# Three moves in a transformer block: first masks, gate rows and first residual each in another place

## Chip, cores and metric

The kernel runs on one core of a Trainium2 chip. The core has a matrix engine (TensorE, "PE"; its weight loads are shown apart as "PEld"), a vector engine (VectorE, "DVE"), a scalar engine (ScalarE, "ACT"), GpSimd ("POOL") and SyncE ("SP"), which here only issues DMAs. Each engine runs its own program; they wait for each other through semaphores. The metric is the device time of one execution in microseconds, as the median of several runs.

## What is computed

One transformer block with layer norm behind each half, on x of 2 sequences x 2048 tokens x 512 features: multi-query causal attention (16 heads of 32, one key and value head), then a mixture of eight experts of which each token takes two.

```python
qkv = einsum('bsd,ed->bse', x, Wqkv_w) + Wqkv_b      # q: 16 heads of 32, k and v: one head each
scores = einsum('bqhd,bkd->bhqk', q, k) / sqrt(32)   # causal mask, softmax over k
out = einsum('bsd,ed->bse', softmax(scores) @ v, out_w) + out_b
x = layernorm(x + out)
top2 = top_k(x @ router_w.T, 2)                      # softmax over the two scores
h = silu(xb @ w1[e]) * (xb @ w3[e])                  # bf16, 8 experts, 128 wide
x = layernorm(x + sum over the two of  weight * (h @ w2[e]))
```

## The kernel before, in words

**Blocks and tiles.** A sequence is worked off in four blocks of 512 tokens (g = 0 to 3), so the program has eight blocks. A block has an attention stage, then an output projection with the first layer norm, in between which the queries, keys and values of the next block are projected, then routing and an expert stage. In attention, a tile is 128 queries of all 16 heads against 128 keys. `TILES` lists them, 136 in a sequence: for query group q first the tile on the diagonal (`FIRST[q]`), which needs the causal mask, then the others. In the first block the tiles are q = 0 (one tile), q = 1 (two), q = 2 (three) and q = 3 (four).

**One tile.** TensorE makes the scores, two halves of two matmuls each, into three PSUM pairs that are used in turn (L1184). ScalarE makes the exponential of each half (L653). GpSimd zeroes both halves of a diagonal tile (`mask`, L520). Two tiles later TensorE multiplies with the values (`times_values`, L1206; the profile has two records for each of its four matmuls, so one tile shows as x8). VectorE adds up a group's tiles (`add`, L833), TensorE forms the denominators from the sums with ones (L1224), VectorE transposes and inverts them and scales the context (`normalise_context`, L882 to L892). ScalarE and VectorE split each context into a high and a low part (L665, L901) for the fp32 products of the output projection (L1037).

**Who waits where, between the sequences.** At a sequence's end VectorE adds the residuals of the last block (`finish_experts`: L906, then statistics L909 and L910), counts `mv_ready`, and waits for GpSimd's reciprocal deviations (`make_rstd`, L545 and L547) to normalise (L916) and so let SyncE store (L434). TensorE meanwhile starts the next sequence: the first tile's scores, then, once the fourth residual is added, the second's and third's, then the first product with the values, which waits for both halves of the first mask. GpSimd's program is a loop over the two sequences (`pool.Fori`); the last `make_rstd` of a sequence is the last thing in its body, so it stands ahead of the next sequence's masks. Its waits in the loop are against register values. The other places where the program asks whether there is a next sequence are branches.

**At a block's end.** TensorE's order is: the last products with the values, output projection of the block's first 128 tokens (`project_out(g, 0)`), the last denominators, projections 1 and 2, keys and values of the next block (L1044, L1049; they wait for GpSimd's low part of x, L565), projection 3, and the queries of the next block. VectorE's order is: the outstanding low parts, `normalise_context` of the last group, its low part, then `finish_attention` with the residuals 0 to 3. Around the attention of a block TensorE has a branch (on a bound that decides whether the scores need a shift); between projection 0 and the last denominators it jumps over the part not taken.

**The expert stage.** TensorE makes two up projections of each of eight experts (`up`, eight matmuls of L1327), turns the gates (L1357), and, once ScalarE has copied them (L689), spreads each expert's row over the partitions (`gate_rows`, one matmul of L1335, two banks in turn). ScalarE applies silu (L683), VectorE multiplies the two projections (`times_linear`, L948, counts `prod_done`), then by the gate row (L995, counts `h_done`). VectorE's order is: products 0 to 3, gated products 0, 1, 2, product 4, gated 3, product 5, gated 4, product 6, gated 5, product 7, gated 6, gated 7. `up` of expert e waits for product e - 3, a gate row for the gated product two before it. The first down projections (`down`, L1342) of the first five experts (`EARLY`) for two token tiles stand in the stage; the others (`LATE`, and all of token tiles 2 and 3) follow behind the next block's first scores, or at once in a sequence's last block. The next block's scores wait for all eight products (`prod_done`), its first exponential for all eight gated products (`h_done`).

## Time and profile before

| | before |
|---|---|
| median of 3 runs | 1117.82 us (1116.93 to 1120.11) |
| the profiled execution | 1121.4 us, span 1119.7 us |
| mean granted TensorE clock | 0.993 |
| PE, busy | 1079.0 us, 96% |
| PEld | 520.2 us, 46% |
| DVE | 888.6 us, 79% |
| ACT | 713.4 us, 64% |
| POOL | 199.3 us, 18% |
| chain of work that ended last | PE 75%, DVE 12%, issue 5% |

Times in the rows are microseconds from the span's start. A row of the timeline has start, duration, engine, line, operation, tile written and tiles read, count, and in brackets the idle time ahead of it with what ended it. Neighbouring operations of one line are merged. "issue" is time in which an engine waited for nothing that the profile shows. The granted clock is a share of 2.4 GHz; 0.50 is the lower level, 1.2 GHz.

### The profile page before, as it was taken

Reading aid. Unit: us, or ns where it says so; the run is one execution under the profiler, and the core shown is the slowest. Engines: PE = TensorE matmul, PEld = TensorE weight load, DVE = VectorE, ACT = ScalarE, POOL = GpSimd, SP = SyncE. Lnnn points to the kernel's source line nnn. Section 1 sums busy time; section 2 is a strip of 40 time slices with the busy share of each in tenths; the row PEclk is TensorE's granted clock in tenths of the full one; section 3 lists DMA queues with packets and bytes.
Section 4 is the critical chain, followed back from the end, with each engine's and each line's share of the span. In section 5 each row is a group of like instructions: output and inputs, shape, how many; then the busy total and the mean of one; then the engine's idle time right before and its main releaser. Section 6 shows DMA issues by size and latency. Waiting matters only on the chain.

```text
span 1119.7 us, 17340 instructions
## 1 busy us (share of the span) xinstructions
PE 1079.0 (96%) x5970; PEld 520.2 (46%) x5994; DVE 888.6 (79%) x1101; ACT 713.4 (64%) x844; POOL 199.3 (18%) x162
## 2 busy tenths in 40 slices
PE   8999999999999999999989999999999999999996
PEld 6365435543337433335634643474333654333462
DVE  4566899779976699987667679976998767898956
ACT  6734785478864498885445457644888447888821
POOL 3520332013110120111032013301211201211000
PEclk9999999999999999999989999999999999999999
DMA  4976401442001622001352353016400152200001
GB/s 146 208 114 141 124 1 40 106 121 38 2 2 53 137 76 38 1 1 39 78 136 75 75 131 76 2 52 138 113 1 1 39 126 65 38 1 2 1 1 38
DMA packets 40331, 72.19 MB, mean 64 GB/s; under 512 B 13969, under 2 KB 14993, under 8 KB 40209
## 3 DMA queue, kind: packets, MB, share of 16 engines
q1 hardware_dynamic: 24624, 56.64, 19.1%
q0 software_dynamic: 13584, 11.54, 7.1%
q10 hardware_dynamic: 2000, 2.51, 0.7%
q8 instruction: 62, 1.02, 0.4%
q14 instruction: 61, 0.49, 0.1%
HBM read 25.58 MB, written 8.39 MB: 30 GB/s over the span
## 4 chain that ended last, share of the span: by engine, by line
PE 75%; DVE 12%; issue 5%; ACT 2%; POOL 2%; DMA 1%; SPq 1%; DVEq 0%; ACTq 0%; POOLq 0%
PE sc L1184 21%; PE bank L1206 19%; PE sc L1037 8%; PE bank L1037 7%; PE sc L1327 7%; DVE psum_k L833 5%; PE sc L1224 3%; PE sc L1342 2%; PE bank L1224 2%; DVE stats L909 2%; POOL prob L520 1%; DVE res L906 1%; PE bank L1335 1%; PE sc L1271 1%; PE bank L1342 1%
## 5 line engine op out<-in xcount | busy, mean ns | idle before, releaser
L653 ACT ACTIVATE prob<-sc 128x1024 f32<-128x1024 f32 x544 | 525.5, 1025 | 133.7 <-PE sc L1184 133.5
L833 DVE TENSOR_TENSOR psum_k<-psum_k,prob 128x2048 f32<-128x2048 f32 x170 | 403.4, 2373 | 4.7
L1184 PE MATMUL sc<-q_st,k_st 128*128 128x512 f32 x1088 | 327.1, 422 | 8.0 <-DVE rden L882 3.8
L1184 PEld LDWEIGHTS sc<-q_st,k_st 128*128 128x128 f32 x1088 | 183.7, 188 | 249.7 <-ACT prob L653 177.3
L1206 PE MATMUL bank<-prob,v_sb 128*32 128x512 f32 x2176 | 288.2, 607 | 3.3 <-POOL prob L520 3.3
L520 POOL TENSOR_SCALAR_AFFINE_SELECT prob<-prob 128x1024 f32<-128x1024 f32 x64 | 112.4, 1798 | 527.7 <-ACT prob L653 527.7
L1327 PE MATMUL sc<-prob,w_sb 128*128 128x512 bf16 x503 | 117.3, 379 | 1.3 <-issue 1.3
L1206 PEld LDWEIGHTS bank<-prob,v_sb 128*32 128x32 f32 x2176 | 44.5, 108 | 107.4 <-issue 89.4
L683 ACT ACTIVATE prob<-sc 128x512 f32<-128x512 f32 x64 | 38.0, 594 | 73.0 <-PE sc L1327 72.9
L833 DVE TENSOR_TENSOR psum_k<-prob 128x2048 f32<-128x2048 f32 x28 | 64.0, 2286 | 20.7 <-POOL prob L520 17.1
L1037 PE MATMUL bank<-q_st,wq_hi 128*128 128x512 f32 x240 | 80.3, 399 | 0.0
L1327 PEld LDWEIGHTS sc<-prob,w_sb 128*128 128x128 bf16 x512 | 49.5, 99 | 62.6 <-issue 5.9
L665 ACT ACTIVATE q_hi<-ctxn 128x512 fp32r<-128x512 f32 x32 | 20.2, 633 | 64.6 <-DVE ctxn L892 64.6
L565 POOL TENSOR_TENSOR q_st<-res,q_st 128x2048 fp32r<-128x2048 f32 x7 | 34.8, 4968 | 126.3 <-ACT q_st L670 126.2
L948 DVE TENSOR_TENSOR prob<-sc,prob 128x512 f32<-128x512 f32 x64 | 43.5, 681 | 12.8 <-ACT prob L683 11.8
L995 DVE TENSOR_TENSOR psum_k<-bank,prob 128x512 bf16<-128x512 f32 x64 | 42.6, 685 | 13.6 <-PE bank L1335 13.6
L1037 PE MATMUL sc<-ow_hi,q_hi 128*128 128x512 f32 x128 | 52.8, 413 | 0.0
L906 DVE TENSOR_TENSOR res<-sc,res 128x512 f32<-128x512 f32 x48 | 32.3, 673 | 24.9 <-PE sc L1342 10.6
L1037 PE MATMUL sc<-ow_hi,q_lo 128*128 128x512 f32 x128 | 51.0, 398 | 0.0
L1037 PE MATMUL sc<-ow_lo,q_hi 128*128 128x512 f32 x128 | 50.8, 397 | 0.0
L1037 PEld LDWEIGHTS bank<-q_st,wq_hi 128*128 128x128 f32 x240 | 45.2, 188 | 9.9
L545 POOL TENSOR_SCALAR rstd<-mv 128x4 f32<-128x4 f32 x16 | 6.2, 389 | 240.6 <-DVE mv L910 240.6
(160 smaller groups left out, 1017.5 us busy)
## 6 DMA issues: line engine op xcount, KB each, us to landing
q_st<-q_hi SPq DMA_DIRECT2D x120, 128.0 KB, 2.4
q_st<-q_lo SPq DMA_DIRECT2D x120, 128.0 KB, 2.4
res<-in_x SPq DMA_DIRECT2D x8, 1024.0 KB, 5.3
res<-ob_sb POOLq DMA_DIRECT2D x8, 1024.0 KB, 9.5
out_x<-res SPq DMA_DIRECT2D x32, 256.0 KB, 2.1
res<-in_xT SPq DMA_DIRECT2D x7, 1024.0 KB, 5.0
w_sb<-in_w POOLq DMA_DIRECT2D x8, 256.0 KB, 9.1
prob<-in_wqkvT ACTq DMA_DIRECT2D x4, 288.0 KB, 6.1
```

The costliest lines, as they stand in the source:

```text
L520: nc.gpsimd.affine_select(out=tile, in_=tile, compare_op=ALU.is_ge, fill=0.0, base=0, pattern=[[0, H // 2], [1, P]], channel_multiplier=-1 ...
L653: nc.scalar.activation(prob[t % NP][:, half * HW:(half + 1) * HW], score_half(q // TB, 2 * t + half).rearrange("p m n -> p (m n)"), ACT.Ex ...
L683: nc.scalar.activation(silu[e % 4], LOW[2 * (e % 3)], ACT.Silu).then_inc(silu_done, 1)
L833: nc.vector.tensor_tensor(acc[:, :], first[:, :], prob[t % NP][:, :], ALU.add).then_inc(add_v, 1)
L906: ins = nc.vector.tensor_tensor(r, src, r, ALU.add)
L948: nc.vector.tensor_tensor(prod[e % 4], LOW[2 * (e % 3) + 1], silu[e % 4], ALU.mult).then_inc(prod_done, 1)
L995: nc.vector.tensor_tensor(hT[:, e, :], gate_bank(e)[:, :], prod[e % 4], ALU.mult).then_inc(h_done, 1)
L1037: last = nc.tensor.matmul(dst, stationary[i][:, c, cols], moving[j][:, c, :], start=(c == 0 and n == 0), stop=(c == DC - 1 and n == 2))
L1184: last = nc.tensor.matmul(dst, k_st[:, k * P:(k + 1) * P], q_st[slot][:, c * HJ:(c + 1) * HJ, at:at + P], start=True, stop=not shift)
L1206: last = nc.tensor.matmul(top[q % 2][c * HD:(c + 1) * HD, :], v_sb[:, k, :], prob[t % NP][:, c * BT:(c + 1) * BT], start=(t == PV_ORDER[FI ...
L1224: last = nc.tensor.matmul(den_bank(q)[c * HD:(c + 1) * HD, :], ones[:, :], src[:, c * BT:(c + 1) * BT], start=(n == 0), stop=(n == len(par ...
L1327: last = nc.tensor.matmul(LOW[2 * (e % 3) + n], w[:, e, c, :], x1Tb[:, c, :], start=(c == 0), stop=(c == DC - 1))
```

## The change

Three moves, and no arithmetic is added or taken away. (1) GpSimd's loop over the sequences is written out, with waits on constants and without branches, and a sequence's last `make_rstd` now stands behind the mask of the next sequence's first tile. (2) In the expert stage TensorE runs the fifth up projection ahead of the wait for the copied gates; every later gate row stands one up projection later, and the last two stand among and behind the early down projections. (3) VectorE does the first residual of a block ahead of `normalise_context` of the last group.

```diff
-            with pool.Fori(0, B) as b:
+            for b in range(B):
...
-                        pool.sem_inc(waited_apart, 1)
...
                         if q == TB * g and g:
-                            make_rstd(2 * g)
+                            make_rstd(b, 2 * g)
+                        if q == 0 and b:
+                            make_rstd(b - 1, 2 * NG)
...
-                    make_rstd(2 * g + 1)
-                make_rstd(2 * NG)
+                    make_rstd(b, 2 * g + 1)
+            make_rstd(B - 1, 2 * NG)
...
+                def first_residual(g):
+
+                    dve.wait_ge(biased, count(b, biased, 16 * (g + 1)))
+                    dve.wait_ge(outproj, count(b, outproj, TB * g + 1))
+                    residual(g, 0, LOW[0], resid1)
+
                 def finish_attention(g):
 
-                    for t in range(TB):
+                    for t in range(1, TB):
...
-                        if t == 0:
-                            dve.wait_ge(biased, count(b, biased, 16 * (g + 1)))
...
+                    first_residual(g)
                     normalise_context(TB * (g + 1) - 1)
...
                     last.then_inc(gates_turned, 1)
+                    up(g, 4)
                     pe.wait_ge(gT_ready, count(b, gT_ready, g + 1))
...
-                    for e in range(4, E):
+                    for e in range(5, E):
                         up(g, e)
-                        gate_rows(g, e - 2)
+                        gate_rows(g, e - 3)
+                    gate_rows(g, E - 3)
+                    pe.wait_ge(prod_done, count(b, prod_done, E * g + 6))
+                    down(g, 0, EARLY[:-1])
                     gate_rows(g, E - 2)
-                    pe.wait_ge(prod_done, count(b, prod_done, E * g + 6))
-                    down(g, 0, EARLY)
+                    down(g, 0, EARLY[-1:])
+                    down(g, 1, EARLY)
                     gate_rows(g, E - 1)
-                    down(g, 1, EARLY)
```

What stands in a row on GpSimd at the end of a sequence, before (the last two `make_rstd`, then the loop's branch back to the mask of the next sequence's first tile; brackets name the semaphores waited for):

```order
L545 TENSOR_SCALAR rstd<-mv 128x4 [waits mv_ready]
L547 TENSOR_TENSOR rstd<-rstd,mhalf 128x4 [waits eps_in]
L543 REGISTER_ALU
L545 TENSOR_SCALAR rstd<-mv 128x4 [waits mv_ready]
L547 TENSOR_TENSOR rstd<-rstd,mhalf 128x4 [waits eps_in]
L512 REGISTER_ALU
L512 COMPARE_AND_BRANCH
```

And now, from the last block's first deviations over the sequences' boundary to the second tile's masks:

```order
L542 TENSOR_SCALAR rstd<-mv 128x4 [waits mv_ready]
L544 TENSOR_TENSOR rstd<-rstd,mhalf 128x4 [waits eps_in]
L519 AFFINE_SELECT prob0<-prob0 128x1024 [waits exped] x2
L542 TENSOR_SCALAR rstd<-mv 128x4 [waits mv_ready]
L544 TENSOR_TENSOR rstd<-rstd,mhalf 128x4 [waits eps_in]
L519 AFFINE_SELECT prob1<-prob1 128x1024 [waits exped] x2
```

The two masks of the first tile have moved ahead of the last reciprocal deviations, and the branch is gone.

TensorE in an expert stage, before, from the turned gates to the first wait for a gated product's bank and on:

```order
L1357 MATMUL bank<-ident_b,ghl 24x128 x3
L1335 MATMUL bank<-gT,pick 128x512 [waits top_ready,gT_ready]
L1335 MATMUL bank<-gT,pick 128x512
L1327 MATMUL sc<-prob,w_sb 128x512 [waits prod_done]
L1327 MATMUL sc<-prob,w_sb 128x512 x7
L1335 MATMUL bank<-gT,pick 128x512 [waits h_done]
L1327 MATMUL sc<-prob,w_sb 128x512 [waits prod_done]
L1327 MATMUL sc<-prob,w_sb 128x512 x7
L1335 MATMUL bank<-gT,pick 128x512 [waits h_done]
```

And now:

```order
L1361 MATMUL bank<-ident_b,ghl 24x128 x3
L1331 MATMUL sc<-prob,w_sb 128x512 [waits prod_done]
L1331 MATMUL sc<-prob,w_sb 128x512 x7
L1339 MATMUL bank<-gT,pick 128x512 [waits top_ready,gT_ready]
L1339 MATMUL bank<-gT,pick 128x512
L1331 MATMUL sc<-prob,w_sb 128x512 [waits prod_done]
L1331 MATMUL sc<-prob,w_sb 128x512 x7
L1339 MATMUL bank<-gT,pick 128x512 [waits h_done]
```

Eight matmuls have moved ahead of the first two gate rows, and each later gate row stands behind one up projection more.

VectorE at the end of the second block's attention, before, from the outstanding low part on:

```order
L901 TENSOR_TENSOR q_lo<-ctxn,q_hi 128x4x128 [waits ctx_high]
L881 REGISTER_ALU [waits ctx_out]
L882 STREAM_TRANSPOSE rden<-bank 128x512 [waits summed]
L884 RECIPROCAL rden_few<-rden 128x16 [waits rden_ready]
L887 STREAM_TRANSPOSE rden<-rden_few 128x512 [waits rden_few_ready]
L890 REGISTER_ALU [waits rden_turned]
L892 TENSOR_TENSOR ctxn<-bank,rden 128x4x128 [waits pv_done]
L901 TENSOR_TENSOR q_lo<-ctxn,q_hi 128x4x128 [waits ctx_high]
L927 REGISTER_ALU [waits outproj]
L906 TENSOR_TENSOR res<-sc,res 128x512 [waits biased]
L909 BN_STATS stats<-res 128x6 [waits resid1]
```

And now:

```order
L900 TENSOR_TENSOR q_lo<-ctxn,q_hi 128x4x128 [waits ctx_high]
L920 REGISTER_ALU
L905 TENSOR_TENSOR res<-sc,res 128x512 [waits outproj,biased]
L908 BN_STATS stats<-res 128x6 [waits resid1]
L817 REGISTER_ALU
L909 BN_AGGR mv<-stats 128x2 [waits v_step]
L880 REGISTER_ALU [waits ctx_out]
L881 STREAM_TRANSPOSE rden<-bank 128x512 [waits summed]
```

The addition with its statistics has moved from behind the last low part to ahead of the last denominators' transposition.

## Rows read from the trace of the kernel before

**Rows 1.** Waits of TensorE, whole span: total us, times, longest us

```profile
PE bank L1335 <- ACT gT L689: 7.0, 8, 0.9
...
PE bank L1206 <- POOL prob L520: 3.3, 3, 2.4
PE bank L1224 <- issue: 3.1, 2, 2.1
```

**Rows 2.** Timeline of the boundary between the sequences

```profile
573.69 5.64 ACT L653 ACTIVATE prob<-sc 128x1024 f32<-128x1024 f32 x6 [5.90 <-PE sc L1184]
...
575.99 0.23 POOL L545 TENSOR_SCALAR rstd<-mv 128x4 f32<-128x4 f32 x1 [38.85 <-DVE mv L910]
...
576.64 0.73 PE L1184 MATMUL sc<-q_st,k_st 128*128 128x512 f32 x2 [0.21 <-ACT prob L653]
577.31 4.77 POOL L520 TENSOR_SCALAR_AFFINE_SELECT prob<-prob 128x1024 f32<-128x1024 f32 x4
577.37 4.99 DVE L916 TENSOR_SCALAR res<-res,mv,rstd 128x512 f32<-128x512 f32 x4 [1.57 <-POOL rstd L547]
...
579.78 1.93 PE L1206 MATMUL bank<-prob,v_sb 128*32 128x512 f32 x8 [2.40 <-POOL prob L520]
...
588.80 1.20 PE L1184 MATMUL sc<-q_st,k_st 128*128 128x512 f32 x4
```

**Rows 3.** Busy time by stretch; PEclk, the granted clock, is the third last

```profile
580.00:583.00 3.00, 3.00 (x11) 1.16 (x4) 2.37 (x2) 0.10 (x1) 3.00 (x3) 0.50 0.61 228
```

**Rows 4.** Timeline, an exponential and the two masks behind it, another block

```profile
228.45 1.94 ACT L653 ACTIVATE prob<-sc 128x1024 f32<-128x1024 f32 x2 [1.15 <-PE sc L1184]
...
229.65 2.15 POOL L520 TENSOR_SCALAR_AFFINE_SELECT prob<-prob 128x1024 f32<-128x1024 f32 x2 [31.43 <-ACT prob L653]
```

**Rows 5.** Timeline, the same work in the first sequence

```profile
37.12 1.06 PE L1206 MATMUL bank<-prob,v_sb 128*32 128x512 f32 x8
...
41.09 1.21 PE L1184 MATMUL sc<-q_st,k_st 128*128 128x512 f32 x4
```

**Rows 6.** Timeline, end of the second block's attention, VectorE and projection 3

```profile
179.48 5.08 DVE L901 TENSOR_TENSOR q_lo<-ctxn,q_hi 128x512 fp32r<-128x512 f32 x1
...
187.75 0.69 DVE L901 TENSOR_TENSOR q_lo<-ctxn,q_hi 128x512 fp32r<-128x512 f32 x1 [0.70 <-ACT q_hi L665]
...
188.36 0.68 DVE L906 TENSOR_TENSOR res<-sc,res 128x512 f32<-128x512 f32 x1
...
189.28 0.19 PEld L1037 LDWEIGHTS sc<-ow_hi,q_hi 128*128 128x128 f32 x1
...
190.03 0.66 DVE L906 TENSOR_TENSOR res<-sc,res 128x512 f32<-128x512 f32 x1
```

**Rows 7.** Timeline, the last block: fourth residual, last gated products, first last residual

```profile
1076.54 0.69 DVE L906 TENSOR_TENSOR res<-sc,res 128x512 f32<-128x512 f32 x1
...
1103.98 1.28 DVE L995 TENSOR_TENSOR psum_k<-bank,prob 128x512 bf16<-128x512 f32 x2
...
1105.94 0.69 DVE L906 TENSOR_TENSOR res<-sc,res 128x512 f32<-128x512 f32 x1 [0.69 <-PE sc L1342]
```

**Rows 8.** Timeline, the second block's expert stage

```profile
215.79 0.68 DVE L948 TENSOR_TENSOR prob<-sc,prob 128x512 f32<-128x512 f32 x1
...
217.22 0.38 PE L1335 MATMUL bank<-gT,pick 128*128 128x512 bf16 x1 [0.91 <-ACT gT L689]
...
224.99 0.59 PE L1335 MATMUL bank<-gT,pick 128*128 128x512 bf16 x2
...
225.48 0.69 DVE L995 TENSOR_TENSOR psum_k<-bank,prob 128x512 bf16<-128x512 f32 x1 [0.65 <-PE bank L1335]
...
226.69 1.28 DVE L995 TENSOR_TENSOR psum_k<-bank,prob 128x512 bf16<-128x512 f32 x2
...
227.63 1.26 PE L1184 MATMUL sc<-q_st,k_st 128*128 128x512 f32 x4
```

**Rows 9.** Chain that ended last, ahead of the first block's last denominators

```profile
60.55 2.06 issue
```

## What the change will do to the time

> **What bounds the kernel now.** I read the page's first part, whose shares stand in the table above, and then the list of waits. TensorE is busy for nearly the whole span and no other engine is near that, so the time is TensorE's work, plus its waits, plus the time it runs at a lower clock. A change that adds and removes no TensorE work can pay only where one of these goes. The waits that the change can touch are few [rows 1]: 7.0 us for the gate rows behind ScalarE's copy of the turned gates (eight times, 0.9 at most) and 3.3 us for a masked tile (three times, 2.4 at most). The third row, 3.1 us of "issue" ahead of a last denominator, is a wait that the profile can't explain; I come back to it in a rival.
>
> The timeline of the boundary between the two sequences [rows 2] shows where the 2.4 us are. GpSimd finds the last deviations ready at 575.99, makes the reciprocal deviation, and only at 577.31 masks the second sequence's first tile, though its exponentials began at 573.69. Beside these masks VectorE's four normalising passes take 4.99 us. TensorE has finished its third tile's scores at 577.37 and starts the first product with the values at 579.78. What follows is the larger half of the price. The window from 580 to 583 [rows 3] has a granted clock of 0.50, which is the 1.2 GHz level: after the idle stretch the clock fell and TensorE worked at half speed. From the start of the first product (579.78) to the start of the sixth tile's scores (588.80) it took 9.02 us.
>
> **Part one: the masks ahead of the deviations.** Two masks take 2.15 us and begin 1.20 us after the first exponential began [rows 4]. From 573.69 that gives 574.89, and the last mask ends at 577.04. TensorE is busy until 577.37, so the mask is no longer late: the product starts at about 577.4 instead of 579.78. How fast does TensorE go from there? In the first sequence the same work from the second value product (37.12) to the sixth tile's scores (41.09) took 3.97 us at full clock [rows 5]. Ahead of that stand one product (a row of 1.06, of which 1.0 to the next) and one tile's scores (1.20 at 588.80, 1.1 to the next), which makes 577.4 + 2.1 + 3.97 = 583.5. ScalarE doesn't stop it: its first six exponentials end at 573.69 + 5.64 = 579.33, and the second product needs the sixth at 579.5. So the sixth tile's scores start at 583.5 where they started at 588.80: **5.3 us**, of which 2.4 are the wait and 2.9 the clock.
>
> What is late next? The reciprocal deviation now stands behind the masks: from 577.1 on it takes the 1.3 us it took before (575.99 to 577.31), and VectorE normalises from 578.5 instead of 577.37. It then shares 2.4 us with the second tile's masks, and I take it to end at 582.0. The transposition of the first denominators follows on VectorE and takes 0.7 us; the sixth tile's scores need it at 583.5. It is hidden by 0.8 us. Rows 2 show the four passes at 4.99 us under four masks and I have only two masks beside them, hence 3.5 us; held throughout it is rival A. The stores of the last block start 1.2 us later and nobody waits for them there. The move also lets GpSimd's program run through without a loop and branches: its waits are on constants. That is worth nothing where it idles, which is most of the time; I cost it at nothing, bounds 0.5 us either way.
>
> **Part two: the first residual ahead of the last context.** In six of the eight blocks VectorE waits for the last denominators anyway and does the residual (three instructions, 1.67 us from one to the next: 188.36 to 190.03 [rows 6]) inside that wait. What it hides is then not needed: the fourth residual waits for TensorE's last output projection. So it neither gains nor costs in five of them; the last block of all comes below. In the second block of the first sequence VectorE isn't early: one subtraction was held for 5.08 us beside GpSimd's (179.48) and it goes on to the last context without a gap [rows 6]. Here the residual pushes the low part of the context from 187.75 to 189.42, ending at about 190.1. TensorE takes it up at 189.28. It waits 0.85 us: **a loss of 0.85**. In the same block of the second sequence VectorE is late too, but TensorE had itself stood still just before and takes the context up well after it is ready, so 1.67 is covered; if it weren't, that block would lose 0.85 too. In the very last block nothing of a next block is projected, and the fourth residual (1076.54 [rows 7]) began as VectorE came free. Now it can begin when the last projection is in, at about 1076.1: **a gain of 0.43**.
>
> The new residual meets GpSimd's long subtraction in four blocks. VectorE's instruction of this form has one operand in PSUM. The rows only show that a subtraction with both operands in SBUF was held (5.08 us against 0.69, [rows 6]). The Trainium skill's "GPSIMD Engine Reference", section 1, Specifications, says that the SBUF interfaces are contended by VectorE instructions in a two-port mode or with two SBUF inputs, which the 5.08 us agree with. By it the residual isn't held.
>
> Were it held all the same, each would end up to 5.08 - 0.69 = 4.4 us late. Most of that is covered by the projections that TensorE has in hand ahead of the last one, so I leave it out of the sum and put a loss of up to 0.9 in one block into the range.
>
> **Part three: gate rows after the fifth up projection.** I worked the second block's stage through by its own rows [rows 8]. TensorE idled until the gate rows (the one at 217.22 is the second of two, so the first began at 217.0), and reached the next scores at 227.63: 50 matmuls in 10.63 us, 0.213 each. Now the fifth up projection comes first. It needs VectorE's second product, which ends at 215.79 + 0.68 = 216.47, so it starts at 216.55. Gate rows two to seven come 1.7 less 0.45 later. VectorE follows each gate row by 0.49 us (224.99 to 225.48) and does six operations of 0.61 after the fifth gate row: the fifth gate row now comes after the eighth up projection (224.2), so VectorE's last gated product ends at 224.2 + 0.49 + 5 x 0.61 + 0.69 = 228.5, against 226.69 + 1.28 = 227.97. TensorE also waits 0.2 us ahead of the down projection, for the sixth product (224.8). Its own end is 216.55 + 10.63 + 0.2 = 227.4 against 227.63. In six stages it goes on with scores, which don't need the late products: **a gain of 0.22 each, 1.3 in all**. In the last block of a sequence the down projection comes at once and needs the last product, 0.6 later than it was: the down projections end **0.43 later at the boundary** and, by the same recurrence from 1103.98 + 1.28 (now 1105.84) to the first residual (1105.94, now 1106.3), **0.35 at the end** [rows 7]. The two rounded ends of this term: 0.9 gained in each of six stages if the wait simply went (5.4 in all), or 0.6 lost in each (3.6) if VectorE's end decided. I take the worked value, since the rows of this stage give both ends of it.
>
> **The sum.** -5.3 + 0.85 - 0.43 - 1.3 + 0.43 + 0.35 = -5.4 us. The profiled execution took 1121.4 (span 1119.7, with 1.7 around it) and should give about 1116.0; it lies 3.6 above the median of the timed runs, 1117.82. From the median the forecast is **1112.4**.
>
> **Rivals.**
> A, the normalising passes are held through everything GpSimd does next. VectorE's passes would then wait out the second tile's masks, the bias transfer's issue (1.4 us) and the third tile's masks, to about 584.6, and the sixth tile's scores come at 585.9: 2.4 lost, 1114.8. For it speaks the 4.99 us in [rows 2]; against it that the passes went on between the masks there. The section of the GPSIMD page named above would allow it.
> B, the expert stage is VectorE's. Scores wait for the eighth product and exponentials for the last gated one, both 0.6 later. If they decide, six stages lose 0.6 where I gain 0.22: +4.9, 1117.3. Against it: after the first scores TensorE has 19 down projections in hand.
> C, the clock falls all the same, from the short waits that stay ahead of the second and third tiles' scores. Then only the wait is gained: 1112.4 + 2.9 = 1115.3. Against it: the third tile's scores, right behind them, ran at their usual pace (two matmuls in 0.73 us, [rows 2]), and the fall came behind the long wait. The Trainium skill's "TensorE: Matmul & The Clock Gate", Part 1, says that idling takes the array to 1.2 GHz and work brings it back, which is what these rows show.
> D, **slower**. Ahead of the last denominators TensorE's program jumps over the branch that it didn't take. In two of eight blocks it stood still there without a releaser, 2.06 us in one of them [rows 9], 3.1 in all [rows 1]. The change moves TensorE's code by a few instructions per block. If each of the eight jumps now cost 2.06, that were 16.5, or 13.4 more: 1125.8. It outweighs the gain from 8.5 us of such stops on. Against it: six blocks show none. The Trainium skill's "Runtime: NRT & Kernel Launch", section Instruction fetch mechanics, has a taken branch outside the fetched window stall for a fetch; it gives no price.
>
> **How the numbers follow.** My sum 0.73, A 0.08, B 0.07, C 0.07, D 0.05. About 0.3% (3.4 us) is what a measurement of this kernel tells from no change, so faster means under 1114.5. The sum's own spread is 1109 to 1114.4: the gate rows' better end would give 1108.3, the stops of D may vanish or double (3.1 us), single-place estimates carry 1 us. A, B and C lie within 0.3%. I give faster 0.74, same 0.21, slower 0.05. The range reaches from 1108.8 to 1116.0, which takes in A and C and leaves out B, D and the sum's far tails.
>
> **What would show it.** In the changed profile: masks at about 574.9 and the reciprocal deviation after them, no wait of TensorE for a mask at the boundary, a clock of 1.0 from 580 to 586, the wait for the gate copy gone and a short one ahead of the fifth up projection and the first down projection, VectorE's last gated product 0.6 later against the stage's start, a wait of 0.8 for the context near 189 us. It is wrong if the clock dips at the boundary, if "issue" grows ahead of the denominators, or if scores wait for VectorE after the experts.

## Result: the changed kernel is slower by half a per cent

| | before | changed |
|---|---|---|
| median of 6 runs | 1120.3 us (1116.93 to 1121.62) | 1126.2 us (1124.09 to 1127.51) |
| span of the profiled execution | 1119.7 us | 1125.6 us |
| mean granted TensorE clock | 0.993 | 0.995 |

The ratio is 1.0055, with a 95% interval of 1.0042 to 1.0068. A gain of 5.4 us to 1112.4 was forecast, and about 6 us were lost; of the rivals only D, at 0.05, had the kernel slower. The page has TensorE busy for 1084.3 us, 5.3 more than before, but that isn't more work: the profile of the kernel before has only 5970 TensorE records where this one has 5994 (both have 5994 weight loads), and 24 matmuls of about 0.2 us make up the difference. So the loss is waits. These are the waits of TensorE in the changed kernel (total us, times, longest):

```profile
PE sc L1188 <- DVE rden L881: 7.6, 6, 3.9
PE sc L1188 <- issue: 3.5, 6, 0.8
PE sc L1188 <- DVE res L905: 2.9, 5, 1.0
...
PE sc L1331 <- DVE prob L951: 1.7, 8, 0.2
```

L1188 is the line of the scores (L1184 before). Both waits that the change was to remove are gone: no row for a mask of 2.4 us, no row for the copied gates [rows 1]. In their place TensorE waits up to 3.9 us for one transposition of the denominators (all six such waits 7.6 us, before 3.8), six times for something that the profile calls "issue" ahead of scores, and five times for a residual.

The boundary between the sequences in the changed kernel (timeline; it answers [rows 2]):

```profile
577.09 7.44 ACT L652 ACTIVATE prob<-sc 128x1024 f32<-128x1024 f32 x8 [6.92 <-PE sc L1188]
...
578.19 2.15 POOL L519 TENSOR_SCALAR_AFFINE_SELECT prob<-prob 128x1024 f32<-128x1024 f32 x2 [38.12 <-ACT prob L652]
...
580.67 1.07 PE L1210 MATMUL bank<-prob,v_sb 128*32 128x512 f32 x8
...
581.68 6.47 DVE L915 TENSOR_SCALAR res<-res,mv,rstd 128x512 f32<-128x512 f32 x4 [2.52 <-POOL rstd L544]
...
589.99 0.72 DVE L881 STREAM_TRANSPOSE rden<-sc 128x512 f32<-128x512 f32 x1 [1.84 <-issue]
...
590.76 1.20 PE L1188 MATMUL sc<-q_st,k_st 128*128 128x512 f32 x4 [3.93 <-DVE rden L881]
...
592.71 1.93 PE L1210 MATMUL bank<-prob,v_sb 128*32 128x512 f32 x8 [0.75 <-DVE ctxn L891]
```

The mask begins 1.10 us after the exponential, and the first product with the values waits for nothing. But the four normalising passes take 6.47 us, VectorE then stands still for 1.84 us, the transposition comes at 589.99, and TensorE waits 3.93 us for it. The product at 592.71 takes 1.93 us where 1.07 is usual: the clock has fallen all the same, now behind the new wait.

The second block's expert stage (timeline; it answers [rows 8]):

```profile
216.69 0.39 PE L1361 MATMUL bank<-ident_b,ghl 128*24 128x128 bf16 x4 [0.18 <-DVE ghl L985]
...
217.30 1.90 PE L1331 MATMUL sc<-prob,w_sb 128*128 128x512 bf16 x8 [0.21 <-DVE prob L951]
...
219.03 0.59 PE L1339 MATMUL bank<-gT,pick 128*128 128x512 bf16 x2
...
227.37 0.68 DVE L951 TENSOR_TENSOR prob<-sc,prob 128x512 f32<-128x512 f32 x1
227.97 1.28 DVE L998 TENSOR_TENSOR psum_k<-bank,prob 128x512 bf16<-128x512 f32 x2
...
228.92 1.17 PE L1188 MATMUL sc<-q_st,k_st 128*128 128x512 f32 x4 [0.49 <-issue]
```

From the turned gates to the next block's first scores there are 228.92 - 216.69 = 12.23 us; in the kernel before 11.71.

**Where the time went.** I took five landmarks in each block and subtracted their times in the two profiles. What each kind of stretch adds in the changed kernel, in us:

| stretch | adds |
|---|---|
| turned gates to the next scores, six stages | 0.87, 0.52, 0.54, 0.97, 0.43, 0.54 = +3.9 |
| turned gates to the first residual, last blocks of the sequences | +0.32, +0.32 |
| last denominators to the transpositions behind the layer norm, second blocks | +0.74, +0.63 |
| the same, last block of all | -0.53 |
| boundary between the sequences, to the last denominators of the block behind it | +0.66 |
| next scores to last denominators, six blocks (before has a stop of 1.07 of its own in one) | -0.18, +0.41, +0.55, -1.64, +0.26, +0.88 = +0.3 |
| the rest | -0.4 |

The boundary, forecast at -5.3, has gained nothing, and the stages have lost where 1.3 was to be gained.

### The profile page after: what moved, and what is told of

It reads as the page before. It is cut to its first block, busy times and chain, and to the rows that moved or that the text cites. A ratio compares the mean times of both kernels' runs of the same rounds, so it can differ in the third digit from the quotient of the medians.

```text
span 1125.6 us, 17176 instructions
## 1 busy us (share of the span) xinstructions
PE 1084.3 (96%) x5994; PEld 517.5 (46%) x5994; DVE 891.6 (79%) x1101; ACT 713.3 (63%) x844; POOL 200.6 (18%) x162
## 4 chain that ended last, share of the span: by engine, by line
PE 68%; DVE 16%; issue 8%; ACT 2%; POOL 2%; DMA 1%; SPq 1%; DVEq 1%; ACTq 0%; POOLq 0%
PE sc L1188 19%; PE bank L1210 17%; DVE psum_k L832 8%; PE bank L1041 7%; PE sc L1041 7%; PE sc L1331 6%; PE sc L1228 3%; PE sc L1346 2%; POOL prob L519 1%; PE bank L1228 1%; ACT prob L652 1%; DVE res L905 1%; PE bank L1339 1%; PE sc L1275 1%; DVE stats L908 1%
## 5 line engine op out<-in xcount | busy, mean ns | idle before, releaser
L1188 PE MATMUL sc<-q_st,k_st 128*128 128x512 f32 x1088 | 325.8, 421 | 16.9 <-DVE rden L881 7.6
L1188 PEld LDWEIGHTS sc<-q_st,k_st 128*128 128x128 f32 x1088 | 182.9, 187 | 259.2 <-ACT prob L652 177.4
L1041 PE MATMUL bank<-q_st,wq_lo 128*128 128x512 f32 x120 | 47.2, 393 | 0.0
```

The source lines that it names most:

```text
L1041: last = nc.tensor.matmul(dst, stationary[i][:, c, cols], moving[j][:, c, :], start=(c == 0 and n == 0), stop=(c == DC - 1 and n == 2))
L1188: last = nc.tensor.matmul(dst, k_st[:, k * P:(k + 1) * P], q_st[slot][:, c * HJ:(c + 1) * HJ, at:at + P], start=True, stop=not shift)
```

## Experiments

All ratios are to the kernel before on the same chip. One unit in the third decimal is 1.1 us.

### The three parts, each alone

Each kernel has one part of the change; "unroll only" writes GpSimd's loop out but leaves the deviations where they were.

```diff
# masks_only: before, with GpSimd's program of the changed kernel
# gates_only: before, with TensorE's experts() of the changed kernel
# resid_only: before, with VectorE's program of the changed kernel
# unroll_only: masks_only, and in GpSimd's program
-                        if q == 0 and b:
-                            make_rstd(b - 1, 2 * NG)
...
-            make_rstd(B - 1, 2 * NG)
+                make_rstd(b, 2 * NG)
```

> The kernel before with GpSimd's part of the change alone (written-out loop, first masks ahead of the last deviations). Theory now (the wait has moved to VectorE): TensorE's wait for the mask at the boundary is gone, but VectorE's four normalising passes take over 6 us under the masks, VectorE then stands about 1.8 us at its own loop's end, and TensorE waits 3 to 4 us for the first denominators' transposition with the clock falling behind it. Total within 1.5 us of the kernel before. Rival (the sum on record): 5.3 us faster, the loss being all in the other two parts.

> GpSimd's loop written out with waits on constants, the order kept as before. Theory: no difference (within 0.5 us), since GpSimd idles most of the time. Rival: the straight program costs or brings something by itself, 1 us or more, which would then be in every kernel that has it.

> The kernel before with the gate rows moved behind the fifth up projection and nothing else. Theory now: the next block's scores start 0.86 us after VectorE's eighth product, in both kernels, and that product comes about 0.5 us later by the stage's own start; eight stages at 0.3 to 0.6 make 3 to 4 us slower. Rival (on record): 1.3 gained in six stages less 0.8 lost in two, 0.5 faster.

> The kernel before with the first residual ahead of the last context and nothing else. Theory (as on record): 0.85 lost in the second block of the first sequence, 0.43 gained in the last block, 0.4 slower in all; up to 0.85 more if the second sequence's second block loses too. Rival: it costs in every block (0.4 each or more, 3 us slower), because the residual is held beside GpSimd's long subtraction.

| kernel | median, us | ratio |
|---|---|---|
| masks_only | 1118.57 | 1.0001 (0.9986 to 1.0016) |
| unroll_only | 1116.84 | 0.9986 (0.9973 to 0.9999) |
| gates_only | 1123.29 | 1.0041 (1.0026 to 1.0056) |
| resid_only | 1122.82 | 1.0026 (1.0012 to 1.0040) |

The parts add up to 1.0068, at the edge of the whole change's interval. So the first part is worth nothing, the second costs 4.6 us and the third 2.9 us. None came out as forecast, and each has its own cause.

### The masks: what holds the first denominators

In the profile of masks_only (timeline) the boundary looks as in the changed kernel, without the other two parts:

```profile
575.26 1.06 PE L1205 MATMUL bank<-prob,v_sb 128*32 128x512 f32 x8
...
576.23 6.47 DVE L915 TENSOR_SCALAR res<-res,mv,rstd 128x512 f32<-128x512 f32 x4 [2.48 <-POOL rstd L544]
...
583.88 0.72 DVE L881 STREAM_TRANSPOSE rden<-sc 128x512 f32<-128x512 f32 x1 [1.18 <-issue]
...
584.65 1.20 PE L1183 MATMUL sc<-q_st,k_st 128*128 128x512 f32 x4 [3.23 <-DVE rden L881]
```

Two suspects: the passes, held to 6.47 us beside GpSimd, and a stop of 1.2 us where VectorE's program has its loop's end. The first kernel writes VectorE's loop out as well; the second also takes the first sequence's last passes out of `finish_experts` and puts them behind the first context of the next sequence.

```diff
-            with dve.Fori(0, B) as b:            # masks_dve_out
+            for b in range(B):
...
                         for q in normalised_at(g, t):    # masks_norm_late
                             normalise_context(q)
+                            if q == 0 and b:
+                                normalise_output(b - 1, NG - 1)
```

> The masks-first kernel with VectorE's loop over the two sequences written out as well. Theory (the stop of 1.2 us between the last normalising pass and the first denominators' transposition is VectorE fetching code behind its loop's branch): the stop goes, TensorE's wait for the transposition falls from 3.2 to about 2 us; the passes still take over 6 us. Total 1 to 2 us faster than masks-first alone. Rival: the stop belongs to the passes or to the guard's branch and stays; no change.

> As masks_dve_out, and VectorE normalises the first sequence's last block behind the second sequence's first context instead of ahead of it. Theory (the masks' gain was eaten by the normalising passes that stand ahead of the transposition): TensorE waits neither for a mask nor for the transposition there, the clock stays at 1.0, and the kernel comes 3 to 5 us under masks_dve_out. Rival: the passes then hold VectorE's first addition, and the wait moves on once more; less than 1.5 us.

masks_dve_out: 1116.74 us, ratio 0.9991 (0.9981 to 1.0001). masks_norm_late: 1114.55 us, 0.9955 (0.9942 to 0.9968), faster than both kernels. The two timelines, masks_dve_out first:

```profile
576.05 6.47 DVE L915 TENSOR_SCALAR res<-res,mv,rstd 128x512 f32<-128x512 f32 x4 [2.52 <-POOL rstd L544]
582.44 0.70 DVE L881 STREAM_TRANSPOSE rden<-sc 128x512 f32<-128x512 f32 x1
```

```profile
577.34 1.06 PE L1216 MATMUL bank<-prob,v_sb 128*32 128x512 f32 x8
...
581.45 0.72 DVE L881 STREAM_TRANSPOSE rden<-sc 128x512 f32<-128x512 f32 x1 [5.62 <-PE sc L1234]
...
583.43 1.19 PE L1194 MATMUL sc<-q_st,k_st 128*128 128x512 f32 x4
583.85 1.91 DVE L1009 TENSOR_SCALAR res<-res,mv,rstd 128x512 f32<-128x512 f32 x4
```

With the loop written out the stop is gone, the passes still take 6.47, and TensorE waits 2.00 us for the transposition instead of 3.23; the time can't be told from that of masks_only (the intervals overlap). Behind the context, with no GpSimd work beside them, the same four passes take 1.91, TensorE waits neither for a mask nor for the transposition, and from the first value product to the sixth tile's scores it takes 583.43 - 577.34 = 6.09 us; the forecast had 583.5 - 577.4 = 6.1. Against before the boundary gains 5.4 us in the profiles (from the first exponential to the sixth tile's scores; sum on record: 5.3). The kernel gains 5.0 us by the ratio and 4.1 by the medians of only five runs against 23. Against masks_dve_out, which differs only in the place of the passes, it is 4.0 us by the ratio, 2.2 by the medians. So most of the forecast's gain exists; what took it was VectorE.

One more thing stands in these profiles. How long the clock stays down is not fixed. The busy time by stretch of unroll_only, where TensorE waits 2.29 us for the mask (before: 2.40), has this; PEclk is the third last column:

```profile
580.00:582.00 2.00, 2.00 (x11) 0.65 (x13) 0.85 (x1) 1.72 (x2) 2.00 (x3) 0.50 0.51 185
582.00:584.00 2.00, 2.00 (x17) 0.46 (x10) 0.04 (x1) 0.22 (x1) 2.00 (x2) 0.76 1.00 243
```

and the same view of the kernel before:

```profile
580.00:582.00 2.00, 2.00 (x9) 0.36 (x2) 2.00 (x2) 0.00 (x0) 2.00 (x2) 0.50 0.57 210
582.00:584.00 2.00, 2.00 (x8) 1.01 (x11) 0.36 (x1) 1.10 (x2) 1.38 (x2) 0.50 0.64 240
584.00:586.00 2.00, 2.00 (x12) 0.40 (x8) 0.00 (x0) 0.84 (x1) 1.90 (x2) 0.50 1.03 192
```

After nearly the same wait the first was at half clock for about 3.4 us (579.6 to 583.0) and the second for about 6.8 (579.3 to 586.0), worth 1.4 us from one to the other. Of the other profiles with the masks left where they were, four had the short form (resid_only among them), three the long one (gates_only among them), and resid_pad16 had no fall at all. So unroll_only's 1.5 us are no gain of writing the loop out that I can claim. The same holds for the forecast: its 2.9 us for the clock were read from one profile with the long form. Against unroll_only's boundary, with the short one, masks_norm_late gains 4.0 us there instead of 5.4.

### The gate rows: who releases the next scores

The first scores of a block wait for the eighth product, 0.86 us behind its end (226.77 to 227.63 before; in the changed kernel 228.05 to 228.92). First idea: the eighth product comes too late, so bring it forward, ahead of the sixth gated product.

```diff
-                        if e == 0 or 3 <= e + 1 < E and e > 2:
+                        if e == 0 or 3 <= e + 1 < E - 1 and e > 2:
                             times_linear(g, max(e + 1, 3))
+                        if e == 5:
+                            dve.wait_ge(h_done, count(b, h_done, E * g + 4))
+                            dve.sem_inc(waited_apart, 1)
+                            times_linear(g, 7)
```

> The gates-only kernel with VectorE's eighth product ahead of the sixth gated product, which makes it 0.6 us earlier and the last gated product no later. Theory (the next block's scores start 0.86 us behind the eighth product): scores start 0.5 to 0.6 us earlier in six stages and the kernel wins about 3 us back, to within 1.5 us of the kernel before. Rival (TensorE's own row of work or the last gated product sets the scores): scores as late as in gates-only, no change.

Measured: 1124.01 us, 1.0047 (1.0030 to 1.0064), no better than gates_only. Its timeline:

```profile
227.70 1.92 DVE L999 TENSOR_TENSOR psum_k<-bank,prob 128x512 bf16<-128x512 f32 x3
...
233.03 0.69 DVE L906 TENSOR_TENSOR res<-sc,res 128x512 f32<-128x512 f32 x1 [3.40 <-issue]
```

```profile
228.44 0.39 PE L1339 MATMUL bank<-gT,pick 128*128 128x512 bf16 x1
229.26 1.16 PE L1188 MATMUL sc<-q_st,k_st 128*128 128x512 f32 x4 [0.43 <-issue]
```

The product is out of the way, but now the last gate row (228.44) comes as its bank is freed by the first of the three gated products (227.70 + 0.69), and the scores again come 0.82 us behind it. From the turned gates to the scores the six stages take as long as in gates_only, within 0.1 us together. (About 2 us of this kernel's profile are another matter: it has the stop of VectorE that the section on the residual describes.) Whatever TensorE's program waits for last in the stage, 0.8 to 0.9 us pass before the scores. What lies between is the value load and the branch around the block's attention. So the next pair moves the wait behind the branch:

```diff
-                    if g:
-                        pe.wait_ge(prod_done, count(b, prod_done, E * g))
                     pe.wait_ge(verdict_ready, count(b, verdict_ready, g + 1))
                     with pe.If(pe.value_load(no_shift[0:1, 0:1]) == 1):
                         ...
+                        if g:
+                            pe.wait_ge(prod_done, count(b, prod_done, E * g))
```

> The kernel before, in which TensorE waits for the eighth product behind the block's branch instead of ahead of it, so that the value is loaded and the branch taken while the products are still running. Theory: the 0.86 us between the end of the eighth product and the next block's first scores (227.63 - 226.77) are the value load, the branch and its fetch; they are hidden now, up to TensorE's own end of the stage (down projections end about 0.1 us before the scores now). Then the scores gain at most 0.1 to 0.3 us in six blocks, 0 to 2 us together, ratio 0.998 to 1.000. Rival: the delay is TensorE's own queue, then nothing moves and the next experiment shows no gain either.

> The gate-row move alone, with the same early branch. Theory: with the gate rows moved the eighth product ends at 227.05 instead of 226.77 and TensorE's own work ends about 0.2 us earlier than in the kernel before; with the branch out of the way the scores no longer follow the product by 0.86 us, so the loss of 0.5 us a stage in six stages (3.5 us in all, ratio 1.0041 of the move alone) goes, and the ratio is 0.998 to 1.001. Rival: it is the moved gate rows' own waits for gated products that cost the time; then the ratio stays at 1.003 to 1.005.

branch_early: 1118.56 us, 0.9995 (0.9984 to 1.0005). gates_branch_early: 1123.02 us, 1.0031 (1.0020 to 1.0043). From the turned gates to the scores both take 11.68 us in this stage (226.26 - 214.58 in the second). Over the six stages the stretch changes by -0.3 and -0.2 us against before, where gates_only has +3.1. The theory of the branch is shown for this stretch, and still the second kernel is slow. Its timeline and its list of waits say where:

```profile
225.86 1.28 DVE L995 TENSOR_TENSOR psum_k<-bank,prob 128x512 bf16<-128x512 f32 x2
...
226.26 1.15 PE L1184 MATMUL sc<-q_st,k_st 128*128 128x512 f32 x4
...
230.70 0.69 DVE L906 TENSOR_TENSOR res<-sc,res 128x512 f32<-128x512 f32 x1 [3.56 <-PE bank L1342]
...
233.08 1.67 PE L1184 MATMUL sc<-q_st,k_st 128*128 128x512 f32 x6 [0.90 <-DVE res L906]
```

```profile
PE sc L1184 <- DVE res L906: 4.2, 7, 0.9
```

The next limit is VectorE's: its first residual stands 3.56 us behind its last gated product, which is itself 0.5 later, and TensorE waits seven times for a residual (branch_early: once, 0.7 us). From the first scores of a block to its second tile's, the six stretches behind an expert stage take 3.0 us longer than in branch_early, most of the 4.0 by which the two kernels differ. VectorE has a branch there, too (`guard`). The last pair leaves it out, together with its other side, the row maxima, which never run for these inputs.

```diff
                 def guard(g):
-                    with dve.If(dve.value_load(no_shift[0:1, 0:1]) == 1):
-                        ...
-                    with dve.Else():
-                        row_maxima(g)
+                    dve.sem_inc(max_read, BLOCK_MAXIMA[g])      # and the other two
```

> The early-branch kernel with the old gate rows, and VectorE's branch ahead of the residuals that finish an expert stage left out with its other side, the row maxima; for these inputs that side never runs, so what VectorE computes is the same. Theory: the 3.0 to 3.2 us between VectorE's last gated product and its first residual are this branch and the fetch behind it, so the first residual follows its down projection at once (about 1.5 us earlier). With the old gate rows TensorE doesn't wait there, so the time stays within 1 us of the early-branch kernel: ratio 0.9985 to 1.0005. Rival: the gap is the wait for the down projections; then the residual stays 3 us behind.

> The same with the gate rows moved. Theory: of the 3.1 us that the moved gate rows still cost with the early branch (ratio 1.0031 against 0.9995, 4.0 us), what comes behind the next block's first scores, TensorE's wait of 0.3 to 1.1 us for VectorE's second residual, goes too, and the kernel is within 1 us of the one with the old gate rows or up to 1 us faster: ratio 0.998 to 1.001. Rival: the loss lies elsewhere in the stage; the ratio stays at 1.002 to 1.004.

Old gate rows: 1115.45 us, 0.9954 (0.9937 to 0.9972). New: 1115.67 us, 0.9970 (0.9959 to 0.9981). In the second one's timeline:

```profile
224.64 1.28 DVE L991 TENSOR_TENSOR psum_k<-bank,prob 128x512 bf16<-128x512 f32 x2
...
226.99 0.69 DVE L902 TENSOR_TENSOR res<-sc,res 128x512 f32<-128x512 f32 x1 [1.07 <-PE sc L1338]
...
230.71 1.74 PE L1180 MATMUL sc<-q_st,k_st 128*128 128x512 f32 x6
```

The residual follows in 1.07 us instead of 3.56, released by its own down projection, and TensorE doesn't wait in this stage (0.9 us in the whole run, twice). The moved gate rows cost 4.6 us with both branches in the way (1.0041), 4.0 with TensorE's moved (1.0031 against 0.9995), and at most 1.8, with intervals that overlap, when VectorE's is gone too; the medians differ by 0.2. They gain in none. What I didn't expect is that the kernel with the old gate rows became 3 to 5 us faster (medians 1118.56 and 1115.45, ratios 0.9995 and 0.9954), where at most 1 us was expected. VectorE's branch had been costing time all along, though no wait for it is in the list. In branch_early the second tile's scores behind the third block's experts start at 388.00, 3.54 us behind the start of the last down projections (384.46). TensorE has just finished these, and the second residual has ended only 0.06 us before (387.28 + 0.66). Without the branch it is 3.27 us, and over the six such places the stretch from a block's first scores to its second tile's is 1.9 us shorter. Leaving the branch out also shortens VectorE's code, and the two weren't separated. The rest isn't placed; the six times of this kernel lie far apart (1111.70 to 1118.88), and the profiled execution is the one of 1118.88.

One difference in the lists is none in time. branch_early's has stops of 0.16 us ahead of eight up projections (1.3 us in all) and 7.0 us of waits for the copied gates, this kernel's has no such stops and 5.4. But branch_early's profile, like that of the kernel before, lacks 24 TensorE records: where its row has seven up projections behind a stop, the full profiles have eight and no stop. The 7.0 us of [rows 1] in the kernel before are 5.4 too.

### The residual: a stop that depends on where the code lies

resid_only shows in both second blocks the wait forecast for one of them, and something not forecast at the start of both fourth blocks, where VectorE adds the third block's expert residuals. The same rows of the changed kernel (timelines):

```profile
190.32 0.50 PE L1041 MATMUL sc<-ow_hi,q_hi 128*128 128x512 f32 x1 [0.47 <-DVE q_lo L900]
```

```profile
387.12 0.69 DVE L908 BATCH_NORM_STATS2 stats<-res 128x6 f32<-128x512 f32 x1
388.89 0.18 DVE L909 BATCH_NORM_AGGREGATE mv<-stats 128x2 f32<-128x6 f32 x1 [1.08 <-issue]
```

VectorE stops for 1.08 us between the statistics and their sum, in the middle of a straight piece of code, and TensorE waits for the residual behind it. It is at the same instruction in both sequences (1.12 and 1.25 us in resid_only), and nowhere in the kernel before. If it is a fetch of code at a fixed place of the program, other code ahead of it moves it. gates_prod_first speaks for the place already. There the first residual isn't moved, VectorE's program only has a few instructions more, and the same stop stands at the same instruction of both sequences (1.00 and 1.02 us), here the second:

```profile
935.54 0.18 DVE L910 BATCH_NORM_AGGREGATE mv<-stats 128x2 f32<-128x6 f32 x1 [1.02 <-issue]
```

The direct test shifts the code:

```diff
             with dve.Fori(0, B) as b:
+                for _ in range(16):
+                    dve.sem_inc(waited_apart, 1)
```

> The residual-only kernel with 16 semaphore increments (no work) put at the top of VectorE's loop, so that all its code lies 16 instructions further on. Theory (the stop of 1.1 to 1.2 us inside the first residual of each sequence's third block is a fetch of code at a fixed place in the program, and moves with it): the stop is gone from that place, and the kernel is 1 to 2 us faster than residual-only. Rival: the stop comes from the moved residual's work itself and stays.

Measured: 1119.66 us, 1.0009 (1.0000 to 1.0018), 1.9 us less than resid_only by the ratios with sixteen instructions that do nothing, though the two intervals overlap. The profile is plainer: the stop is no longer in the residual of either sequence. Another one stands at the sequences' boundary:

```profile
586.30 0.72 DVE L884 STREAM_TRANSPOSE rden<-sc 128x512 f32<-128x512 f32 x1 [3.93 <-issue]
```

Part of this idle time is a real wait, since TensorE ends these denominators only at 583.81; TensorE then waits 1.1 us for the transposition and 0.8 for the context. What is left of the loss, 1 us, is what the other stretches give: 0.78 and 0.62 us more in the second blocks, 0.41 less in the last. So the stop depends on what code lies ahead of it, and the moved residual's own work is not its cause. That it is a fetch of code is inferred: no row names one.

### Put together

masks_norm_late with the early branch, and the first residual ahead of the last context in the very last block alone; then the same with the gate rows moved.

```diff
+                    if b == B - 1 and g + 1 == NG:
+                        first_residual(g)
                     normalise_context(TB * (g + 1) - 1)
```

> Masks ahead of the deviations, both loops written out, normalising passes behind the second sequence's first context, early branch, the first residual ahead of the last context in the very last block alone, gate rows as before. Theory: the late normalising run's 5.0 us, 0.4 for the last block and 0 to 2 for the branch: 1111 to 1114, ratio 0.9925 to 0.995. Rival (code position costs as much again): no better than 0.9955.

> The same with the gate rows moved. Theory of the branch: 0.2 us less in each of six stages, 1.3 in all less what it costs at the boundary and the end (0.8), so within 1 us of the kernel with the old gate rows. Rival (gated products' waits cost): 3 to 4 us slower than it.

best_old_gates: 1114.29 us, 0.9957 (0.9943 to 0.9971); best_new_gates: 1117.15 us, 0.9987 (0.9976 to 0.9998). The first is no faster than masks_norm_late, so the early branch and the last block's residual added nothing that can be measured, and the expectation of 0.9925 to 0.995 was missed. The gate rows cost 3 us more on top, as the rival said. VectorE's branch is still in there, and the six stretches from a block's first scores to its second tile's, in which it lies, are 2.8 us longer than with the old gate rows. masks_norm_late stays the kernel to take; its passes' new place together with the left-out branch of VectorE (no_guard_old_gates, 0.9954, for these inputs only) was not tried.

## Why the prediction was wrong, step by step

- **The masks (-5.3 forecast, 0 measured alone).** Start of the mask, no wait for it and the pace afterwards were right (6.1 forecast, 6.09 once VectorE was out of the way). The step that failed is "hidden by 0.8 us". The passes were put at 3.5 us, since only two masks lie beside them; they took 6.47, and the bias transfer's issue and the third tile's masks lay beside them too. That is rival A's mechanism, which I gave 0.08 against [rows 2], where the passes took 4.99 under four masks: I read that row as "the passes went on between the masks" instead of as 1.25 us a pass. A's own price was too small, 2.4. TensorE waited 3.93 us. I had left out VectorE's stop at its loop's end (1.18 and 1.84), which in the kernel before lay under an idle 4.46 us, and the clock, which fell to 0.50 behind the new wait as it had behind the old one. The Trainium skill's "GPSIMD Engine Reference", section 1, Specifications, names such contention for VectorE instructions in a two-port mode or with two SBUF inputs; 1.91 us alone and 6.47 beside GpSimd agree if the passes are in that mode, which no row shows.
- **The residual (+0.85 - 0.43 forecast, +2.9 measured alone).** TensorE's wait for the context was 0.47 us, in both second blocks, and these blocks grew by 0.74 and 0.63 us up to the layer norm: about the 0.85 forecast for one of them. The step that failed first is the cover that I named for the second sequence; it wasn't there. The last block's gain was right (0.43 forecast, 0.41 in resid_only, 0.53 in the changed kernel). The residual wasn't held beside GpSimd (0.68 us), as forecast. The missing term is VectorE's stop behind the third blocks' experts: in resid_only the stretch to the second tile's scores grew by 0.74 and 1.07 us there. With the second blocks (0.74 and 0.66) and the last block's gain these make 2.8 of the 2.9 us.
- **The gate rows (-1.3 + 0.43 + 0.35 forecast, +4.6 alone).** The recurrence for VectorE held: the fifth up projection came 0.61 us behind the turned gates (0.63 forecast), the last gated product ended 12.56 us behind them (12.6), and the sequences' ends cost 0.32 and 0.32. What failed is "its own end is 216.55 + 10.63 + 0.2", taken as the start of the scores. That is 11.5 us behind the turned gates; the changed kernel took 12.23. The scores wait for the eighth product and then 0.86 us for the branch. In the kernel before that path ended within 0.03 us of TensorE's own (11.71 against 11.68 with the branch early), so nothing showed it, and every delay of the product by 0.5 went straight through. This is rival B, at 0.5 us instead of 0.6. Even with the branch out of the way nothing is gained: 11.68 us with the new gate rows as with the old. The 19 down projections "in hand" were the argument against B; VectorE's branch used them up (3.0 us in six stages of gates_branch_early, and TensorE's seven waits there are two without it). I had A and B as rivals with 0.08 and 0.07, of which at most one is true; their mechanisms came together.
- **Rival D.** The jump ahead of the last denominators is not it: its "issue" fell to 2.0 us in one block (before: 3.1 in two [rows 1]). Over the profiles of all kernels it is 2.0 to 4.5 us in one to three blocks, and what decides that stays open. But its root, engines that stop where the program branches, is what the other parts ran into, on other jumps than the one I looked at. The Trainium skill's "Runtime: NRT & Kernel Launch", section Instruction fetch mechanics, says that a taken branch outside the fetched window stalls for a fetch; the stops behind VectorE's loop end and guard, and their going away with the branches, agree.

## What to carry to other kernels

A wait that the profile doesn't show may be a tie: before moving work, list every wait of the next stage, add the branch behind it, and see which of them end within a few tenths of the engine's own work. Work that is moved under GpSimd must be priced at what such an instruction takes there, for everything that GpSimd has queued, and if nobody needs it soon, it is better put behind the step that somebody needs. A step that sits between two engines' branches is the last place to add half a microsecond.

## What was new about the hardware

- Four fp32 passes with per-row scalars took 1.91 us with GpSimd idle, 4.99 under four masks, 6.47 under masks and a DMA's issue: a factor of 3.4.
- From the release of TensorE's last wait over a value load and a branch to the first matmul: 0.82 to 0.90 us in four kernels. On VectorE, from the end of the last instruction ahead of such a branch to the first behind it: 2.7 to 3.6 us in fourteen kernels, against 1.0 to 1.6 in the two without the branch, where the next down projection ends the wait.
- Straight code stops too: 1.00 to 1.25 us on VectorE at one instruction in three kernels, in both sequences; with sixteen instructions more ahead of it the stop was gone from there.
- After a wait of 2.3 to 2.4 us the granted clock was at 0.50 for 3.4 us in some profiles, 6.8 in others and not at all in one, with the same code at this place.
